# The mask of later keys: from a TensorE product ahead of the scores to a VectorE multiplication behind the exponentials

## The reference

```python
x = x + tanh(g_xattn) * xattn(layernorm(x), ctx, ctx, W, b, mask)
x = x + tanh(g_ffn) * ffn(layernorm(x), ...)

def xattn(q, k, v, W, b, mask):        # 16 heads of 16, 256 queries, 77 keys for each block
    scores = einsum('bhqd,bhkd->bhqk', qh, kh) / 4
    scores = where(causal == 1 or pad == 1, -inf, scores)   # causal: key index > query index
    return (softmax(scores) @ vh) @ W.T + b
```

## Time and profile before

| what | value |
|---|---|
| median of 3 runs | 1141.14 us (1137.15 to 1141.66) |
| the profiled execution's own time | 1138.31 us |
| its span, first to last instruction | 1136.6 us |
| TensorE busy | 1084.2 us, 95% of the span |
| VectorE busy | 818.2 us, 72% |
| ScalarE busy | 472.3 us, 42% |
| GpSimd busy | 520.0 us, 46% |
| mean granted TensorE clock | 0.986 |

### The profile page before, as it was taken

How to read it: one execution, slowest core, us unless ns; L and a number is a source line. 1 busy time by engine, 2 the same in 40 slices (tenths; PEclk the granted TensorE clock), 3 DMA queues, 4 the chain that set the end, 5 groups by cost and what they waited for, 6 DMA issues and landing times.

```text
span 1136.6 us, 22381 instructions
## 1 busy us (share of the span) xinstructions
PE 1084.2 (95%) x7411; PEld 908.4 (80%) x7411; DVE 818.2 (72%) x1810; ACT 472.3 (42%) x722; POOL 520.0 (46%) x644
## 2 busy tenths in 40 slices
PE   5689999999999999999999999999999999999997
PEld 3467888888788787788888777888887888888886
DVE  7757786886876876877878676557544688888886
ACT  4565556555555555655555432233221111111111
POOL 5334447457357456465563534000001566666564
PEclk8989999999999999999999999999999899999999
DMA  8975748666765764766666112687652554555451
GB/s 157 244 159 120 147 102 129 135 126 102 146 137 123 119 146 106 113 141 128 99 128 145 29 55 74 209 260 242 214 173 104 163 157 154 163 166 150 148 175 64
DMA packets 106162, 160.64 MB, mean 141 GB/s; under 512 B 28828, under 2 KB 70718, under 8 KB 106048
## 3 DMA queue, kind: packets, MB, share of 16 engines
q1 hardware_dynamic: 94276, 121.18, 46.8%
q0 software_dynamic: 11776, 38.03, 11.1%
HBM read 75.24 MB, written 52.10 MB: 112 GB/s over the span
## 4 chain that ended last, share of the span: by engine, by line
PE 71%; issue 11%; DVE 7%; POOL 6%; DMA 3%; ACT 2%; SPq 1%; POOLq 0%; DVEq 0%; ACTq 0%
PE ps L764 16%; PE ps L811 12%; PE ps L709 7%; PE ps L726 7%; PE ps L813 6%; PE ps L631 4%; PE ps L796 3%; PE ps L619 3%; PE ps L662 2%; POOL tab_dram L1471 2%; PE ps L585 2%; PE ps L589 2%; POOL x L1447 2%; DMA regr<-regr 2%; PE ps L640 1%
## 5 line engine op out<-in xcount | busy, mean ns | idle before, releaser
L811 PE MATMUL ps<-regr,gh 128*128 x600 | 221.6, 407 | 0.2 <-issue 0.2
L888 ACT ACTIVATE Pt<-ps,pbias 77x1024 f32<-77x1024 f32 x128 | 141.6, 1106 | 98.2 <-PE ps L619 96.8
L813 PE MATMUL ps<-regr,gl 128*128 x600 | 170.0, 283 | 0.0
L811 PEld LDWEIGHTS ps<-regr,gh 128*128 128x128 f32 x600 | 113.8, 190 | 23.9 <-issue 0.6
L978 ACT ACTIVATE gh<-ps 128x512 fp32r<-128x512 f32 x75 | 44.8, 599 | 204.9 <-PE ps L796 204.9
L1189 DVE TENSOR_REDUCE mneg<-ps 128x8 f32<-128x616 f32 x128 | 100.4, 792 | 21.3 <-PE ps L589 21.1
L813 PEld LDWEIGHTS ps<-regr,gl 128*128 128x128 f32 x600 | 114.0, 190 | 0.0
L709 PE MATMUL ps<-x2h,winh 128*128 128x512 f32 x256 | 108.2, 423 | 0.6 <-DVE OHR L1093 0.6
L1379 POOL TENSOR_TENSOR gl<-gf,gh 128x512 fp32r<-128x512 f32 x64 | 82.7, 1293 | 42.8 <-ACT gh L850 42.6
L1447 POOL TENSOR_TENSOR x<-x,regf 128x512 f32<-128x512 f32 x32 | 41.1, 1285 | 132.7 <-DMA x<-in_x 132.7
L709 PE MATMUL ps<-x2h,winl 128*128 128x512 f32 x256 | 100.6, 393 | 0.0
(11 more groups left out here) (201 smaller groups left out, 2652.9 us busy)
## 6 DMA issues: line engine op xcount, KB each, us to landing
regr<-regr SPq DMA_DIRECT2D x96, 256.0 KB, 5.9
y_dram<-Pt SPq DMA_DIRECT2D x64, 256.0 KB, 2.4
regf<-in_x SPq DMA_DIRECT2D x32, 256.0 KB, 4.3
x<-in_x SPq DMA_DIRECT2D x32, 256.0 KB, 7.2
y_dram<-res SPq DMA_DIRECT2D x32, 256.0 KB, 2.4
regr<-regr SPq DMA_DIRECT2D x96, 77.0 KB, 6.9
x_dram<-x2h SPq DMA_DIRECT2D x14, 512.0 KB, 3.0
x_dram<-x2l SPq DMA_DIRECT2D x14, 512.0 KB, 3.8
```

Source lines behind the costliest of these rows:

```text
L811: e.matmul(o, gh2[:, k % 3, fc, :], w2v[:, bass.ds(val, 1), fc, :, :].rearrange("p o h d -> p (o h) d"), start=fc == 0, stop=False, skip_g ...
L813: m = e.matmul(o[:, 0, :], gl2[:, k % 3, fc, :], w2v[:, bass.ds(val, 1), fc, 0, :].rearrange("p o d -> p (o d)"), start=False, stop=fc == ...
L888: e.activation(Pt[0:K, 4 * k:4 * k + 4, :].rearrange("k (n j) t -> k n (j t)", n=2), bank_of["sc", b, k][0:K, :, :], ACT.Exp, bias=pbias[: ...
```

## The change

TensorE no longer adds the mask. `cauT` becomes a triangle of ones and zeros. A new stage, causal, runs on VectorE twice in each block: for eight heads at a time it takes the corner `Pt[0:77, 8 heads, 0:77]`, limits it to 3e38 and multiplies it with the triangle, in place. Causal 0 stands in slot 5, behind the exponentials of scores 1; causal 1 in slot 8, behind those of scores 3 and ahead of moments. Values 0 and 1 stand in slot 9 and wait for the new semaphore `cz` where they waited for `P`.

```diff
-        put(i - 2, ((1, "scores", 0), (3, "scores", 1), (5, "scores", 2), (7, "scores", 3), (8, "values", 0), (8, "values", 1),
+        put(i - 2, ((1, "scores", 0), (3, "scores", 1), (5, "causal", 0), (5, "scores", 2), (7, "scores", 3),
+                    (8, "causal", 1), (9, "values", 0), (9, "values", 1),
                     (5 if i < 6 else 11, "load_x1", 0), (11, "att", 0)))
...
                     for n in range(2):
-                        e.matmul(pair[0:K, n, :].rearrange("k (j t) -> k j t", j=2)[:, :, 0:K], identb[0:K, 0:K],
-                                 cauT[:, :].unsqueeze(1).broadcast_to([K, 2, K]), start=True, stop=False, skip_group_check=True)
-                    for n in range(2):
                         p, bk = 2 * k + n, pair[:, n, :]
                         for j in range(2):
                             m = e.matmul(bk[0:K, j * S:(j + 1) * S], Kst[:, ks, j, p % 4, 2 * g + p // 4, :],
-                                         Xs[:, h, p % 4, p // 4, :], start=False, stop=j == 1, skip_group_check=True)
+                                         Xs[:, h, p % 4, p // 4, :], start=True, stop=True)
                     m.then_inc(s["sc"], 1)
                 elif stage_ == "values":
...
-                    e.wait_ge(s["P"], 4 * b + 2 * k + 2)
+                    e.wait_ge(s["cz"], 2 * b + k + 1)
...
+                elif stage_ == "causal":
+                    if b == 0 and k == 0:
+                        e.wait_ge(s["gcon"], GCON["cauT"])
+                    e.wait_ge(s["P"], 4 * b + 2 * k + 2)
+                    v = Pt[0:K, 8 * k:8 * k + 8, 0:K]
+                    e.scalar_tensor_tensor(v, v, BIG, cauT[:, :].unsqueeze(1).broadcast_to([K, 8, K]), ALU.min,
+                                           ALU.mult).then_inc(s["cz"], 1)
...
-            e.memset(cauT[:, :], 0.0).then_inc(s["gcon"], 1)
+            e.memset(cauT[:, :], 1.0).then_inc(s["gcon"], 1)
...
-            e.affine_select(out=cauT[:, :], in_=cauT[:, :], compare_op=ALU.is_ge, fill=NEGP, base=0,
+            e.affine_select(out=cauT[:, :], in_=cauT[:, :], compare_op=ALU.is_ge, fill=0.0, base=0,
                             pattern=[[1, K]], channel_multiplier=-1).then_inc(s["gcon"], 1)
```

More of the change, by code:

```diff
@@ L22 @@
 NEG = -1e30
-NEGP = -3e38
+BIG = 3e38
 NEGB = -2.5e38
@@ L205, in build @@
             "tg khi xn xTh mT P ks1 OT aTh x2h lgT t gh re1 re2 sh wh t2 gh2 "
-            "dcon lo klo mom0 mom1 xTl pad mx mhi mlo rden att aTl x1 n2 x2l LG u f res sl rv rdif rsub rcc roh rslot rrec "
+            "dcon lo cz klo mom0 mom1 xTl pad mx mhi mlo rden att aTl x1 n2 x2l LG u f res sl rv rdif rsub rcc roh rslot rrec "
             "nt en tk ti ei wl u2 f2 gl2 acc0 acc1 "
@@ L603, in tensor @@
                             e.wait_ge(s["ks1"], 1)
-                            e.wait_ge(s["gcon"], GCON["cauT"])
+                            e.wait_ge(s["dcon"], DCON["idb"])
                         if b == G:
```

## The result

The changed kernel takes 1259.97 us (median of 6 runs, 1253.94 to 1263.39) against 1139.26 us for the kernel before (6 runs): a ratio of 1.1033, 95% interval 1.0995 to 1.107. It is slower by 10.3%, inside the range of 1190 to 1262 but near its upper end; the forecast was 1229. The profiled execution took 1263.39 us against 1138.31.

The account below looks back on a forecast made before the run. TensorE, busy in 95% of the span, was taken as the bound; stalls 67, blocks 0 to 5 4 and clock 17 made 88 us on 1138.3: 1226, plus 2.8 to the median: 1229 us, range 1190 to 1262.

Parts of the forecast that it names:

- Causal at 0.80 us: Each of the two new VectorE instructions a block takes 0.80 us, estimated from VectorE's products of two SBUF tensors.
- the stall of block 14: TensorE at values 1: VectorE's lag 2.44 plus 0.80, 0.80 and 0.06, together 4.10 us.
- The term of the stalls: TensorE waiting at values 1 for causal 1: 5.2 us a pair, 13 pairs in blocks 6 to 31, 67 us.
- the term of the clock: TensorE at half rate for some 2.7 us of work after even stalls: 12 x 1.4 = 17 us.
- The legs add up, through x1: Even and odd stalls add, since x1's load, which starts VectorE's even chain, stands behind the odd block's values 1.
- Near causal 0 and 1 of these four blocks GpSimd is mostly between its long rows, so I count none: Blocks 14 to 17: no hold of causal by GpSimd counted; if a third of 52 waited 1.0 us, 17 us more.
- Values 0 waits for causal 0 [...] no cost: Values 0 on TensorE: causal 0 is right behind proj, VectorE through at 321.98, values 0 starting at 326.65; nothing counted.
- The odd stalls, 1 to 2 us, lie about the second row, and I count nothing: TensorE's clock after odd blocks' stalls: a 1.82 us wait had left it at 1.00, so no loss counted.
- Blocks 0 to 5: First six blocks: more cover by slot order and DMA waits, half the odd price, 4 us (0 to 12).
- I count the last pair like the others: Last of the 13 pairs in blocks 6 to 31: same price as the others, 5.2 us.
- isn't the bound by its sum: VectorE's load rises by 1.6 us in some 20 us, from 79% to 87%, so its total doesn't bound.
- The rival that VectorE is in time: VectorE reaches causal 1 before TensorE wants values 1, so the masks' 16.6 us come through: 1124 us; chance 0.05.

Follow-up runs that it names:

- wait_no_work: Kernel before, mask matmuls kept, plus a one-column VectorE memset at the places of causal 0 and 1, for which values wait: 1206.65 us, ratio 1.054.
- x1_early: Changed kernel with load_x1 in slot 7 in place of 11: 1237.23 us, ratio 1.085 to the kernel before.
- early_causal_early_x1: Changed kernel with causal 1 in slot 7 ahead of norm2 and load_x1 in slot 7: 1180.95 us, ratio 1.032 to the kernel before.
- no_lock: Changed kernel with causal replaced by a same-length reduction of one SBUF tensor into a spare tile, mask left out: 1247.68 us, ratio 1.091 to the kernel before.
- clock_filler: Changed kernel, TensorE repeating the matmuls of values 0 three times more in even blocks from 6 on: 1241.29 us, ratio 1.090 to the kernel before.
- work_no_wait: Changed kernel, causal run on a spare tile, values waiting only for the exponentials, mask left out: 1182.53 us, ratio 1.034 to the kernel before.
- no_mask: Changed kernel without the causal stage, so no mask at all, values waiting for the exponentials: 1136.59 us, ratio 0.995 to the kernel before.

## Why the prediction was right, and where it was too small

- **The mechanism is shown.** TensorE stands at values 1 until VectorE gets to its place in the order. The wait alone costs 5.4% (wait_no_work), the wait rows name L1179, and moving causal 1 ahead of norm2 takes half of the loss away.
- **Causal at 0.80 us** was right (0.79 median), and so was the stall of block 14: 4.10 forecast, a wait of 4.55 us where 0.17 had been, which is 4.38 more with the masks' 0.26 in it. In block 15 the forecast wait was 1.90, the row has 1.74; in block 17 1.22 and 1.05. For block 16 it was 3.65, and values 0 and values 1 waited 1.30 and 3.23, 4.53 together where 0.21 had been. Block 14's closeness is partly luck. Causal 0 took 1.23 us there and L1204 1.14 (0.19 in block 16), both longer than counted; but the forecast had taken over a norm2 of 1.69 us from the trace of before, and that was 0.72 in the changed kernel.
- **The term of the stalls was right in its sum, the term of the clock was too small.** In blocks 6 to 31 TensorE waited 87 us for L1179, 84 more than before for L994; less 13.5 us for the masks' 104 stages that makes 70, where 67 were forecast. These blocks grew by 110 us, so about 40 are left, mostly the clock, where 17 were forecast (estimate, from the starts of values 1 and the waits). With 12 us in place of 4 in blocks 0 to 5 and 3 behind the phase, that is the 125 us measured against 88.
- **The legs add up, through x1**: shown by x1_early (-1.8% of the kernel before) and by early_causal_early_x1.
- **"Near causal 0 and 1 of these four blocks GpSimd is mostly between its long rows, so I count none"** is a step that failed. Causal 0 was held in the even blocks: 1.23 us in block 14 and 2.48 in block 16, where it also ate up the 1.50 us of norm2's wait that the forecast counted on, and made values 0 wait for 1.30 us, which "Values 0 waits for causal 0 [...] no cost" had at nothing. With it went about 14 us (no_lock). I took the hold for GpSimd's long rows alone; in block 16 causal 0 stood still during an indirect DMA (L1476) of GpSimd as well. The trace of before had these rows already. Causal 0's place there is behind the statistics of x, at 303.26 us in block 14 and 344.14 in block 16, and GpSimd's rows lie right across both:

```profile
302.46 1.28 POOL L1379 TENSOR_TENSOR gl<-gf,gh 128x512 fp32r<-128x512 f32 x1
...
343.55 1.00 POOL L1471 DMA_INDIRECT tab_dram<-rec,slot  x1 [0.16 <-issue]
344.57 1.30 POOL L1379 TENSOR_TENSOR gl<-gf,gh 128x512 fp32r<-128x512 f32 x1
```

"No cost" at values 0 was read off block 15. In block 16 values 0 started only 0.6 us after the earliest end of causal 0:

```profile
345.52 1.07 PE L631 MATMUL ps<-Pt,regf 77*32 77x256 f32 x16
```

- **"The odd stalls, 1 to 2 us, lie about the second row, and I count nothing"** failed, and the even ones were sized too small. The stall of 1.74 us in block 15 is followed by the lower clock; the one of 4.55 us by 5 us or more of it, where 2.7 were counted. From 160 to 710 us the mean clock of the changed kernel is 0.91, which is 18% of 550 us, 99 us, at half rate, and can cost up to 50 us, where 17 were counted. clock_filler gave about 15 back.
- **Blocks 0 to 5** were put at 4 us; values 1 of block 5 comes 12.3 us later than before, the upper bound given. TensorE waits 15.2 us for L1179 there, ten times, where it had waited 3.5 us for the exponentials. The mean clock from 0 to 140 us is 0.83, 0.93 before. Why was not tried by a run.
- **"I count the last pair like the others"** was too little too: values 1 of blocks 29, 30 and 31 wait for 3.81, 6.94 and 3.50 us.
- **VectorE's load "isn't the bound by its sum"** is right by its sum and hid a price: work_no_wait loses 4% against no_mask with VectorE busy for 78% of the time (160 to 680 us). I treated the stall as one of the new wait, while the old wait for L994 stood behind causal 0 with no slack left.
- **The rival that VectorE is in time** had 17 us for the masks. Even with no causal mask at all only 5.7 us come through, and 12 with an early x1.

## What to carry to other kernels

When an instruction is added to an engine that looks a fifth idle, find the first wait of the busy engine that stands behind the new instruction, and read how far the two engines are apart there; a wait of 0.2 us that repeats is a tie without slack, not a trifle. The gain from removed work has to be read at the same places. Read the other engines' rows at the very place of the new instruction, in each kind of block. A stall of TensorE can cost more than its own length, through the lower clock behind it; here those of 1.7 us and more did. And the place in an in-order queue can be worth more than the duration: moving one instruction ahead of others that take 1 to 1.6 us was worth 57 us.

## What the runs showed of the hardware

- TensorE's granted clock fell to 0.50 after a wait of 1.74 us in the changed kernel, while it stayed at 1.00 after one of 1.82 us in the kernel before. The length of the wait alone doesn't decide. After waits near 1.05 us (blocks 9, 13, 17 and 25) it stayed at 1.00. After those of 1.72 to 1.74 us in blocks 7, 11, 15, 23 and 27 the mean of the next 3.2 us or so was 0.50 to 0.74.
- Repeating matmuls in a stall, with no other use, made the kernel faster: 1.090 in place of 1.103 (clock_filler).
- A VectorE instruction with two SBUF inputs was held not only during GpSimd's long rows: causal 0 of block 16 stood from about 399.4 to 401.2, across the end of an indirect DMA (to 399.85) and the whole row after it, which began at 399.87. So GpSimd took the next turn, not VectorE. In no_lock the reduction with one SBUF input took 792 ns at most.
